# A decoder layer in which GpSimd takes part of the expert routing, with a power for the reciprocal

## The reference

```
x = layernorm(x + self_attention(x))                # 16 heads of 8, learned relative positions
x = layernorm(x + cross_attention(x, ctx_1024))     # 16 heads of 8, causal
x = layernorm(x + ffn(x))                           # 64 experts, 8 of them per token, and a shared one
```

```
scores = sigmoid(x @ router_w.T)                    # 64 experts
sfc    = scores + correction_bias                   # in 8 groups of 8 experts
group score = sum of the two largest sfc of a group; the 4 best groups are kept
masked = sfc in the kept groups, 0 elsewhere;  the 8 largest experts are chosen
tw     = scores[chosen] / (scores[chosen].sum() + 1e-20) * 2.5
out    = sum over chosen e of tw[e] * (relu(x @ up[e])**2 @ down[e])  +  the shared expert
```

## Time and profile before

| | us |
|---|---|
| median of three runs | 278.6 (278.17 to 279.26) |
| the profiled execution, in all | 278.31 |
| its span | 276.5 |
| granted clock of TensorE over the span | 0.984 |

### The profile page before, as it was taken

How to read it: one execution, slowest core, us unless ns; L and a number is a source line. 1 busy time by engine, 2 the same in 40 slices (tenths; PEclk the granted TensorE clock), 3 DMA queues, 4 the chain that set the end, 5 groups by cost and what they waited for, 6 DMA issues and landing times.

```text
span 276.5 us, 5995 instructions
## 1 busy us (share of the span) xinstructions
PE 255.8 (92%) x1920; PEld 203.9 (74%) x1920; DVE 202.8 (73%) x563; ACT 215.9 (78%) x572; POOL 142.3 (51%) x137
## 2 busy tenths in 40 slices
PE   6989999999999999999897689999998999999991
PEld 5579998788888877777574454768886888788860
DVE  2698737778888889998999984588994556855534
ACT  8571660889999998999998777788897887698861
POOL 5009001500111149763655005388998998699982
PEclk9999999999999999999999979999999999999996
DMA  6709320396732325866660002976691896597201
GB/s 127 179 16 410 108 85 0 98 229 224 234 113 77 85 76 120 187 171 174 171 172 21 1 2 81 233 184 189 166 222 33 194 247 170 147 233 205 63 0 38
DMA packets 52259, 37.94 MB, mean 137 GB/s; under 512 B 15810, under 2 KB 43140, under 8 KB 52228
## 3 DMA queue, kind: packets, MB, share of 16 engines
q1 hardware_dynamic: 52228, 37.57, 51.7%
HBM read 30.48 MB, written 7.08 MB: 136 GB/s over the span
## 4 chain that ended last, share of the span: by engine, by line
PE 66%; DVE 12%; POOL 5%; SPq 5%; issue 4%; DMA 4%; ACT 2%; DVEq 0%; POOLq 0%; ACTq 0%
PE bank L746 27%; PE bank L728 10%; PE bank L763 5%; PE bank L781 5%; PE bank L791 3%; POOL unit_lo L646 3%; PE bank L769 3%; DVE neg_max L1250 3%; SPq L463 2%; PE bank L674 2%; DMA qc_dram<-q_lo 2%; PE bank L880 2%; SPq L459 2%; PE bank L669 1%; PE bank L681 1%
## 5 line engine op out<-in xcount | busy, mean ns | idle before, releaser
L646 POOL TENSOR_TENSOR unit_lo<-unit,unit_hi 128x512 fp32r<-128x512 f32 x68 | 86.6, 1293 | 31.4 <-ACT unit_hi L1098 30.4
L1006 ACT ACTIVATE probs<-bank,neg_max 128x128 f32<-128x128 f32 x224 | 64.2, 397 | 4.0 <-DVE neg_max L1250 3.8
L1381 DVE SCALAR_TENSOR_TENSOR scaled<-bank,roots 128x512 f32<-128x512 f32 x64 | 43.7, 686 | 27.1 <-PE bank L746 22.8
L1097 ACT ACTIVATE unit<-scaled 128x512 f32<-128x512 f32 x68 | 42.9, 630 | 17.3 <-DVE scaled L1381 15.6
L1250 DVE TENSOR_REDUCE neg_max<-bank 128x4 f32<-128x512 f32 x56 | 38.3, 684 | 10.4 <-PE bank L769 9.6
L781 PE MATMUL bank<-ident,probs 128*128 128x128 f32 x256 | 39.5, 277 | 3.1 <-ACT probs L1006 3.1
L1098 ACT ACTIVATE unit_hi<-scaled 128x512 fp32r<-128x512 f32 x68 | 41.9, 617 | 0.0
L781 PEld LDWEIGHTS bank<-ident,probs 128*128 128x128 f32 x256 | 30.3, 142 | 8.7 <-ACT probs L1006 5.7
L769 PE MATMUL bank<-k_bd,q_stk 128*128 128x512 f32 x64 | 34.0, 532 | 0.0
L728 PE MATMUL bank<-spread,rel_t 128*128 128x128 f32 x256 | 28.9, 275 | 0.0
L728 PEld LDWEIGHTS bank<-spread,rel_t 128*128 128x128 f32 x256 | 28.7, 192 | 0.1
(11 more groups left out here) (214 smaller groups left out, 481.9 us busy)
## 6 DMA issues: line engine op xcount, KB each, us to landing
roots<-root_dram SPq DMA_DIRECT2D x60, 256.0 KB, 4.7
q_stk<-q_dram SPq DMA_DIRECT2D x16, 128.0 KB, 3.1
k_bd<-k_dram SPq DMA_DIRECT2D x32, 64.0 KB, 2.4
incoming<-in_L_ffn_up_w SPq DMA_DIRECT2D x4, 512.0 KB, 4.5
q_stk<-qc_dram SPq DMA_DIRECT2D x16, 128.0 KB, 3.3
k_bd<-kc_dram SPq DMA_DIRECT2D x32, 64.0 KB, 2.6
incoming<-in_L_ffn_down_w SPq DMA_DIRECT2D x4, 512.0 KB, 4.3
k_dram<-k_hi SPq DMA_DIRECT2D x2, 512.0 KB, 3.4
```

The costliest lines, as they stand in the source:

```text
L646: nc.gpsimd.tensor_tensor(unit_lo[:, k % R], unit[:, k % 3], unit_hi[:, k % R], ALU.subtract).then_inc(lo_ready, 1)
L1006: last = nc.scalar.activation(probs[:, U % 3, h4 * L:(h4 + 1) * L], ps[BS[U % 3]][:, h4 * L:(h4 + 1) * L], ACT.Exp, bias=neg_max[:, U % 4, ...
L1097: nc.scalar.activation(unit[:, k % 3], scaled[:, k % 3], ACT.Square)
L1381: ins = nc.vector.scalar_tensor_tensor(scaled[:, k % 3], h, 0.0, roots[:, n % ROOT_RING, c % ROOTS], ALU.max, ALU.mult)
```

## The change

- The parts of routing that are products or sums over 128 x 64 tiles move from VectorE to GpSimd for batches 0 and 1, in a new function `route_share`: one plus the exponential, the bias, masked, weight, comb and the Newton step (in which the factor 0.5 moves to ScalarE's copy). VectorE keeps the maxima, the replacements and the small sums, and waits at parts 3, 10 and 12 for GpSimd; GpSimd waits for VectorE at masked, weight and comb. `PART_AT` gives these two batches new steps.
- GpSimd makes the score as a tensor_tensor power: r_one to the power of a column of minus ones. VectorE's reciprocal is gone for these batches.
- The order of rows in pos becomes sequence, then head. w_hi and w_lo become w_parts, one slot per piece, each over the rows of one sequence. A split of piece B waits for the scores of sequence B alone, and the pieces are loaded and split during the self-attention; the load of piece b is now behind gather b + 2.
- EARLY is 2 in place of 4, so two chunks get their roots by matmul, and set 1 comes from DRAM.
- The layer norm is one scalar_tensor_tensor, with the deviation broadcast as a second operand, in place of a tensor_scalar with two per-partition scalars.
- ScalarE copies the turned weights before it reads the logits of that step.

```diff
-EARLY = 2 * ROOTS
+EARLY = ROOTS
...
+PART_AT = (0, 0, 0, 1, 1, 1, 1, 2, 2, 3, 3, 3, 4, 4, 5)
...
 def part_step(q, part):
 
+    if q < 2:
+        return ROUTE0[q] + PART_AT[part]
     return ROUTE0[q] + int(min(part, PARTS - 2) / BATCHES[q][1]) + (part == PARTS - 1)
...
-        w_hi = sb("w_hi", [128, 2, E * IM], F32R)
-        w_lo = sb("w_lo", [128, 2, E * IM], F32R)
+        w_parts = sb("w_parts", [128, NB, 2, 2 * E * IM // NB], F32R)
...
                 gather(B)
+                if 2 <= B - 2 < NB:
+                    load_piece(B - 2)
...
-                if 2 <= B - 7 < NB:
-                    load_piece(B - 7)
...
-                if B >= NB:
-                    b = B - NB
...
-                        pool.wait_ge(scores_ready, NU)
...
-                    way, cols = piece(b)
-                    pool.wait_ge(ld[f"piece{b % 2}"], 16 * (b // 2 + 1))
-                    nc.gpsimd.tensor_copy(w_hi[:, way, cols], incoming[:, b % 2]).then_inc(w_high, 1)
-                    pool.wait_ge(w_high, b + 1)
-                    nc.gpsimd.tensor_tensor(w_lo[:, way, cols], incoming[:, b % 2], w_hi[:, way, cols],
...
+                    pool.wait_ge(ld[f"piece{B % 2}"], 16 * (B // 2 + 1))
+                    pool.wait_ge(scores_ready, NG * (B + 1))
+                    nc.gpsimd.tensor_copy(w_parts[:, B, 0], incoming[:, B % 2]).then_inc(w_high, 1)
+                    pool.wait_ge(w_high, B + 1)
+                    nc.gpsimd.tensor_tensor(w_parts[:, B, 1], incoming[:, B % 2], w_parts[:, B, 0],
                                             ALU.subtract).then_inc(w_split, 1)
...
+            def route_share(q):
+
+                seqs = BATCHES[q][0]
...
+                pool.wait_ge(logit_exp, seqs[-1] + 1)
...
+                nc.gpsimd.tensor_scalar(r_one[:, at, :], r_exp[:, at, :], 1.0, None, ALU.add).then_inc(one_made, 1)
+                pool.wait_ge(one_made, q + 1)
+                link(nc.gpsimd.tensor_tensor(score[:, at, :], r_one[:, at, :],
+                                             minus_one[:, :].unsqueeze(2).broadcast_to([128, size, E]), ALU.pow))
+                nc.gpsimd.tensor_tensor(biased[:, at, :], score[:, at, :],
+                                        corr_row[:, :].unsqueeze(1).broadcast_to([128, size, E]), ALU.add)\
+                    .then_inc(biased_made, 1)
+                pool.wait_ge(keep_made, q + 1)
+                pool.wait_ge(biased_made, q + 1)
+                nc.gpsimd.tensor_tensor(masked[:, at, :].rearrange("p n (g e) -> p (n g) e", g=EG),
+                                        biased[:, at, :].rearrange("p n (g e) -> p (n g) e", g=EG),
+                                        gkeep[:, at, :].rearrange("p n g -> p (n g)").unsqueeze(2)
+                                        .broadcast_to([128, size * EG, ES]), ALU.mult).then_inc(masked_made, 1)
+                pool.wait_ge(chosen_made, q + 1)
+                nc.gpsimd.tensor_tensor(weight[:, at, :], score[:, at, :], chosen[:, at, :], ALU.mult)\
+                    .then_inc(weight_made, 1)
+                pool.wait_ge(wrec_made, q + 1)
+                pool.wait_ge(weight_made, q + 1)
+                nc.gpsimd.tensor_tensor(comb[:, at, :], weight[:, at, :],
+                                        wrec[:, at].unsqueeze(2).broadcast_to([128, size, E]), ALU.mult)\
+                    .then_inc(comb_made, 1)
+                base, inverse = first_root_tiles(q)
+                pool.wait_ge(root_newton, q + 1)
+                link(nc.gpsimd.tensor_tensor(root_sum[:, at, :], comb[:, at, :], inverse, ALU.mult))
+                link(nc.gpsimd.tensor_tensor(inverse, root_sum[:, at, :], base, ALU.add))
+                nc.gpsimd.tensor_tensor(root[:, at, :], inverse, chosen[:, at, :], ALU.mult).then_inc(root_made, 1)
+
+            for q in range(2):
+                for b in BATCHES[q][0]:
+                    tokens_low(b)
+                route_share(q)
...
-                        row = head_of(g, h4) * NB + b
+                        row = b * H + head_of(g, h4)
...
-                nc.scalar.copy(root_t[:, f * HT:(f + 1) * HT], ps[(4, BN)[f]][0:E, :]).then_inc(ct_out, 1)
+                nc.scalar.mul(root_t[:, f * HT:(f + 1) * HT], ps[(4, BN)[f]][0:E, :], (0.5, 1.0)[f]).then_inc(ct_out, 1)
...
+                if s - 1 in CT:
+                    weights_out(CT.index(s - 1))
                 if at_step(s, USE) is not None:
                     queries_out(at_step(s, USE))
                 if s in ROOTS_AT:
                     first_roots(ROOTS_AT.index(s))
-                if s - 1 in CT:
-                    weights_out(CT.index(s - 1))
...
-                nc.vector.tensor_scalar(dst, res[:, B % 2, :], moments[:, B % 2, 0:1], rstd[:, B % 2, :],
-                                        ALU.subtract, ALU.mult).then_inc(x_norm, 1)
+                nc.vector.scalar_tensor_tensor(dst, res[:, B % 2, :], moments[:, B % 2, 0:1],
+                                               rstd[:, B % 2, :].broadcast_to([128, D]),
+                                               ALU.subtract, ALU.mult).then_inc(x_norm, 1)
...
-                if part == 0:
+                shared_out = q < 2
+                if part == 0 and not shared_out:
...
+                if part == 1 and not shared_out:
+                    dve.wait_ge(exp_read, q - 1)
                     mark(nc.vector.reciprocal(sig, one))
-                if part == 2:
+                if part == 3 and shared_out:
+                    dve.wait_ge(biased_made, q + 1)
+                if part == 2 and not shared_out:
                     mark(nc.vector.tensor_tensor(biased[:, all_n, :], sig,
                                                  corr_row[:, :].unsqueeze(1).broadcast_to([128, size, E]), ALU.add))
...
                 if part == 10:
+                    if shared_out:
+                        dve.wait_ge(masked_made, q + 1)
                     for n in range(first, first + size):
...
                 if part == 12:
 
-                    link(nc.vector.tensor_tensor(weighted, sig, chosen[:, all_n, :], ALU.mult))
+                    if shared_out:
+                        dve.wait_ge(weight_made, q + 1)
+                    else:
+                        link(nc.vector.tensor_tensor(weighted, sig, chosen[:, all_n, :], ALU.mult))
                     mark(nc.vector.tensor_reduce(sums, weighted, AX.X, ALU.add))
                 if part == 13:
                     link(nc.vector.tensor_scalar(wsum1[:, all_n], sums, 1e-20, None, ALU.add))
                     link(nc.vector.reciprocal(wrec[:, all_n], wsum1[:, all_n]))
+                    if shared_out:
+                        nc.vector.tensor_scalar(wrec[:, all_n], wrec[:, all_n], ROUTE_SCALE, None, ALU.mult)\
+                            .then_inc(wrec_made, 1)
+                        return
...
-                if part == 14:
+                if part == 14 and not shared_out:
```

More of the change, by code:

```diff
@@ L118, in piece, with expert_weights @@
     return n // (NB // 2), slice(n % (NB // 2) * size, (n % (NB // 2) + 1) * size)
+def expert_weights(w_parts, way, c):
+    per_piece = 2 * NPAIR // NB
+    cols = slice(c % per_piece * 128, (c % per_piece + 1) * 128)
+    return [w_parts[:, way * NB // 2 + c // per_piece, part, cols] for part in range(2)]
 def h_bank(k):
@@ L363, in decoder_layer @@
         exp_read = sem("exp_read")
+        one_made = sem("one_made")
+        biased_made = sem("biased_made")
+        keep_made = sem("keep_made")
+        masked_made = sem("masked_made")
+        chosen_made = sem("chosen_made")
+        weight_made = sem("weight_made")
+        wrec_made = sem("wrec_made")
+        comb_made = sem("comb_made")
+        root_made = sem("root_made")
         comb_ready = sem("comb_ready")
@@ L393, in decoder_layer, with pos_rows @@
         block = ctx.enter_context(nc.Block())
+        def pos_rows(n):
+            return pos[:, :, 4 * n:4 * n + 4].rearrange("p (b h) i -> p h b i", h=H)
         def bank_of(task):
@@ L633, in _ @@
[L633 to L647 removed]
+                if B == 0:
+                    pool.wait_ge(ld["sup"], 16)
+                    pool.wait_ge(ld["sdn"], 16)
+                    nc.gpsimd.tensor_copy(sh_hi[:, :, :], shared[:, :, :]).then_inc(shared_high, 1)
+                    pool.wait_ge(shared_high, 1)
+                    nc.gpsimd.tensor_tensor(sh_lo[:, :, :], shared[:, :, :], sh_hi[:, :, :], ALU.subtract)
@@ new lines, in _ @@
+            for q in range(2):
+                for b in BATCHES[q][0]:
+                    tokens_low(b)
+                route_share(q)
+            for k in range(2 * CH):
+                if k == REST2:
+                    for b in range(HB, NB):
+                        tokens_low(b)
+                pool.wait_ge(hi_ready, k + 1)
+                if k >= R:
+                    pool.wait_ge(down_done, k - R + 1)
+                nc.gpsimd.tensor_tensor(unit_lo[:, k % R], unit[:, k % 3], unit_hi[:, k % R],
```

(26 more changed lines are left out.)

55 lines of the change are left out of this document (24 added, 31 removed).

## The result

The changed kernel takes 317.8 us (316.6 to 318.3, four runs), the kernel before on the same chip 278.4: a ratio of 1.139 (95% interval 1.135 to 1.142). The prediction was 275.8 us, with a range of 271 to 288.

What follows compares the result with a forecast made beforehand. TensorE was taken to bound the first attention, VectorE the stretch from 100.5 to 165 us, with ScalarE close behind. 278.3 - 1.0 + 1.6 - 4.5 - 1.7 + 2.8 = 275.5, against the median 275.8; range 271 to 288.

Steps and rivals of the forecast that it cites:

- 3. The power: GpSimd's score in the first two routing batches: power of 3.9 us, stalling VectorE 1.4 us per batch, 2.8 us lost.
- my own formula: Whole kernel: 273.0 us without a stall, plus P - 2.5 in each of two batches, P being the power's time.
- The slack: Before VectorE wants biased in step 52: a power of up to 2.5 us is hidden.
- 2. The routing: Maximum of step 51 to that of step 63: from 27.2 to 22.7 us, 4.5 gained, bounds 3 and 5.6.
- ScalarE's floor: Routing steps 51 to 63: ScalarE's exponentials need 1.80 us a step, so 21.6 us for twelve.
- my first paragraph: Bounds by stretch: a lighter VectorE pays little up to about 147 us and much from there on.
- The wait for masked: Routing step +3: VectorE stands for GpSimd's masked, 0.46 us and two hand-overs of some 0.1; 1.3 us for two batches.
- The tail of 4.9 us: Maximum of step 63 to the transpose of the roots: 4.9 us after the change, 4.96 before.
- 1. The pieces: Weight pieces split during the first attention: 1.0 us gained after 100 us, 1.6 us lost to held norms.
- The waits for k_bd: TensorE after 100 us: 1.7 us in two waits before the change, none expected after it.
- 4. The sets: Two root spreads of 1.05 us fewer on TensorE, one set from DRAM instead: 1.7 us gained, bounds 0 and 2.1.
- the power's length: Rival at the wait for biased, steps 52 and 60: power beyond 5.3 us, 284 us at P = 8; chance 0.35.

Runs made afterwards that it cites:

- recip: Changed kernel with VectorE's reciprocal in place of GpSimd's power for the first two batches; ratio 1.001 to the kernel before, from the four faster of ten times.
- before_pieces: Kernel before plus only the weight pieces loaded and split during the first attention, with the new layout of weights and pos; ratio 1.001 to the kernel before.
- before_early2: Kernel before with EARLY = 2 as its only edit; ratio 0.994 to the kernel before, 1.8 us faster.
- recip_early4: Changed kernel with VectorE's reciprocal in place of the power, and EARLY 4 again; ratio 1.010 to the kernel before.
- act_spread: Changed kernel with ScalarE's exp(-ln(1 + e)) in place of the power, and routing parts spread otherwise over the steps; 278.5 us, ratio 0.995 to the kernel before.
- pow_each: Changed kernel with GpSimd's power made for each sequence once its exponential is there, not per batch; 309.2 us, ratio 1.107 to the kernel before.
- the probe: Kernel before plus six GpSimd powers whose results nothing uses, of 16, 32 and 64 columns; 281.35 us in its one run.
- recip_oldnorm: Changed kernel with VectorE's reciprocal in place of the power, and the layer norm as the old tensor_scalar; ratio 1.019 to the kernel before.

## Why the prediction was wrong

The mechanism was named right, stall and place, and its sign was among the rivals; the size wasn't. The step that failed is the third.

**3. The power.** Predicted 3.9 us with bounds of 0.46 and 9, and so a stall of 2.8 us; measured 20.75 and 37.9. The value came from factors (3.3 times a simple operation, twice), and the upper bound from a composition, a logarithm, a product and an exponential as 25 operations of 0.34 us. Neither is a bound: no row showed a power, nor any operation of GpSimd of more than two simple ones. I called 9 an end and gave the whole forecast a range that stopped at 10. With 20.75 in my own formula, 273.0 + 2 x (20.75 - 2.5), the kernel would be at 309.5. The slack was near what I said: the two waits are 37.9 us together, 36.5 by the formula. The sentence from the Trainium skill (GPSIMD Engine Reference, "Performance pitfalls for Q7 kernels") gave 8.5 us as an estimate, since I had put in 20 dependent operations; the trace disagrees with that count by a factor of 2.4. It was the nearer of my two figures. Here the power took 45 times a multiplication of the same size (20.75 against 0.46 us); whether it is such a chain of dependent operations, no run shows.

**2. The routing.** Predicted 4.5 us of gain, measured none: 26.9 to 28.6 us for the twelve steps, where the old routing takes 26.4 to 28.7. VectorE did lose the work: 28.2 us busy between 130 and 165 in recip, 32.6 before. I summed work over twelve steps and compared it with ScalarE's sum. But each step has its own bound: one with 3.2 us of VectorE's work and a 0.59 us wait takes 3.8, and the next ones, at the chain's 1.4 us, give nothing back. The two halves show it. Steps 51 to 59 took 14.6 us before, 1.8 a step, which is what I had called ScalarE's floor; there nothing was to be gained, as my first paragraph says of the time up to 147 us, and in the changed placing they take 16.9 to 19.0. Steps 59 to 63 went from 12.6 to 9.6 in recip. Spread, the two are 14.9 and 8.8 us, 23.7 together, near my 22.7. A smaller slip: the 0.89 us for one plus the exponential is the mean of 1.55 (held by a split) and 0.22, so the hold is counted here and in term 1 too. The wait for masked was 0.59 us, as counted (0.65). The tail of 4.9 us was right (4.74) for the parts placed as in the change.

**1. The pieces.** Predicted 1.0 us gained and 1.6 lost. In before_pieces 2.0 are lost and some gained, and the kernel's time is the same. In the changed kernel steps 0 to 31 take 1.5 us longer (52.39 against 50.91), and one norm there was held, 1.80 us in place of 0.34, until the split beside it was over (GpSimd's row first):

```profile
81.78 2.37 POOL L654 TENSOR_TENSOR w_parts<-incoming,w_parts 128x1024 fp32r<-128x1024 f32 x1
```
```profile
82.49 1.80 DVE L1346 SCALAR_TENSOR_TENSOR x_tok<-res,moments,rstd 128x128 f32<-128x128 f32 x1
```

In the earlier trace rows no norm of that phase took more than 0.34. The waits for k_bd after 100 us, which the forecast had vanish, are still 1.3 us in three, before 1.7 in two.

**4. The sets.** Predicted 1.7 us. Measured 1.8 (before_early2) and 2.5 (recip against recip_early4). Right, and the only part of the change that by itself made the kernel faster. In the changed kernel it doesn't show: from the transpose to the end it takes the 111.7 us of before, with a granted clock of 0.50 in the first 2 us and 0.77 in the next 2, where the kernel before had 1.00. In act_spread and pow_each, at 1.00 all the way, it is 110.5, 1.3 us under before.

The changed kernel's 317.8 against the formula's 309.5: 1.4 us by the longer waits, and 6 by the gain of the rest that isn't there (recip at the time of before, where 273.0 stood for it). About 1 us is left, which may be the clock after the stalls and after the roots; it wasn't tried alone.

The chances: I gave the power's length 0.35, the largest rival. Its price was capped by my bound of 9 us, and the range of 288 (a power of 10) with it.

## What to carry to other kernels

Where no row shows an operation, a composition of other rows is no upper bound; the honest range is open above, and one look at 16 columns of it in idle time settles the matter before anything hangs on it. Moving work to an engine that is idle on average pays only if its queue is free at that very time, and hand-overs in a loop of short steps must be counted per step, not over the phase. A mixed change should be tried part by part: here the moved pieces and the routing as placed gave nothing, and the smallest part, two spreads fewer, was alone 0.6% faster.

## What the hardware showed beside that

- The power took 20.753 and 20.756 us in the changed kernel, 10.56 for 64 columns, and in the probe 2.90 to 3.30 for 16 with other bases and an exponent of 0.5: its time goes by columns, 0.16 us each, and hardly by values.
- In the changed kernel a norm of two SBUF tiles that starts at 137.76, beside a running power, takes 0.34 us, and so does the old form in the probe. Beside the 128x1024 subtraction both forms are held until it ends. The Trainium skill (SBUF — State Buffer, "Who interferes with whom") has a VectorE instruction with two SBUF inputs and a GpSimd instruction that reads SBUF exclude each other for the whole instruction; by that rule the norm beside the power would have taken 18 us, and the trace doesn't agree. Which GpSimd operations hold VectorE and which don't, these runs show for these two only.
- In recip_oldnorm TensorE ran at 1.2 GHz in the 10 us after the roots (0.50 granted), and the way from their transpose to the end was 115.2 us. In act_spread, with the same number of spreads and 2.4 GHz (1.00), it was 110.5. In the kernel before the half clock lay ahead of the transpose (0.50 from 159 to 162 us) and the granted clock was 1.00 behind it.
